# A gated delta-rule mixer ahead of a local transformer: the inversion of the delta groups split by rows over two engines, and their products rewritten with fewer, wider matmuls

## What is computed

```
T = strict_lower(-kb @ k^T) per chunk            # 32 x 32
for i in 1..31: T[i, :i] += T[i] @ T             # inverse of a triangle
T = T + I;  u = T @ v;  w = T @ kb
for each of 8 chunks:
    attn = lower(q @ k^T)
    u_i = u - w @ S
    o   = q @ S + attn @ u_i
    S   = lam * S + k^T @ u_i
stats(short), stats(long), stats(delta), stats(v)   # mean, variance, max, norm
p = floor(softmax(mlp([x, stats]) / temp))
o = p0*short + p1*long + p2*delta + p3*v
out = rms_norm(o, norm_w) @ Wo
```

## Time and profile before

| | us |
|---|---|
| median of three runs | 4124.85 |
| profiled execution | 4126.29 |
| its span | 4124.5 |
| PE busy | 3701.8 |
| DVE busy | 3111.3 |
| ACT busy | 2917.1 |
| POOL busy | 2318.9 |

### The profile page before, as it was taken

How to read it: one execution, slowest core, us unless ns; L and a number is a source line. 1 busy time by engine, 2 the same in 40 slices (tenths; PEclk the granted TensorE clock), 3 DMA queues, 4 the chain that set the end, 5 groups by cost and what they waited for, 6 DMA issues and landing times.

```text
span 4124.5 us, 143879 instructions
## 1 busy us (share of the span) xinstructions
PE 3701.8 (90%) x60178; PEld 3028.5 (73%) x60178; DVE 3111.3 (75%) x5783; ACT 2917.1 (71%) x5403; POOL 2318.9 (56%) x2139
## 2 busy tenths in 40 slices
PE   4747544799999999999999999999999999999998
PEld 3636533588887888878888888888788887888776
DVE  4385684777888777787777888777877878877873
ACT  2322121688888888888888888888888888888885
POOL 0000000666666666666666666666766666666662
PEclk9766565899999999999999999999999999999999
DMA  2000000343333333334333333333343333343332
GB/s 61 23 29 2 13 12 10 82 107 84 93 89 99 106 88 88 90 90 118 90 90 90 90 101 107 90 89 91 86 117 89 89 88 89 99 106 94 98 94 53
DMA packets 149484, 332.27 MB, mean 81 GB/s; under 512 B 17632, under 2 KB 27616, under 8 KB 147168
## 3 DMA queue, kind: packets, MB, share of 16 engines
q1 hardware_dynamic: 148832, 322.95, 29.6%
HBM read 218.02 MB, written 104.86 MB: 78 GB/s over the span
## 4 chain that ended last, share of the span: by engine, by line
PE 50%; ACT 17%; POOL 9%; issue 5%; DVE 2%; POOLq 0%; ACTq 0%; DVEq 0%
PE bank L1577 13%; PE bank L1694 8%; PE bank L1614 7%; PE bank L1667 7%; PE bank L1636 5%; PE bank L1682 3%; PE bank L1744 3%; ACT L1238 3%; ACT L1236 3%; POOL qk L1039 3%; PE bank L1651 2%; ACT gate L1236 2%; POOL qk L1049 2%; POOL pr L1058 2%; ACT qT L1132 1%
## 5 line engine op out<-in xcount | busy, mean ns | idle before, releaser
L1039 POOL TENSOR_TENSOR qk<-rot_a,rot_b 128x512 f32<-128x512 f32 x768 | 987.5, 1286 | 692.9 <-PE bank L1614 649.0
L1049 POOL TENSOR_TENSOR qk<-qk,rn 128x512 f32<-128x512 f32 x768 | 800.7, 1053 | 71.0 <-DVE rn L1456 71.0
L1377 DVE TENSOR_TENSOR rot_a<-bank,rot 128x512 f32<-128x512 f32 x768 | 531.1, 691 | 368.4 <-PE bank L1577 338.6
L1577 PE MATMUL bank<-w_hi,xs_hi 128*128 128x512 f32 x1152 | 571.8, 496 | 39.7 <-POOL xs_lo L1029 20.4
L1121 ACT ACTIVATE sq<-bank 128x512 f32<-128x512 f32 x768 | 458.9, 598 | 181.7 <-DVE rot_b L1384 179.2
L1058 POOL TENSOR_TENSOR pr<-pr,prec 128x512 f32<-128x512 f32 x384 | 400.5, 1043 | 290.4 <-DVE prec L1421 290.4
L1392 DVE TENSOR_REDUCE ss<-sq 128x8 f32<-128x512 f32 x768 | 513.9, 669 | 52.6 <-ACT sq L1121 52.4
L1384 DVE TENSOR_TENSOR rot_b<-bank,rot 128x512 f32<-128x512 f32 x768 | 522.9, 681 | 0.0
L1614 PE MATMUL bank<-ident,qk 128*128 128x128 f32 x3072 | 465.4, 274 | 53.8 <-ACT qT L1132 50.9
L1614 PEld LDWEIGHTS bank<-ident,qk 128*128 128x128 f32 x3072 | 368.5, 141 | 159.4 <-issue 92.2
L1577 PE MATMUL bank<-w_lo,xs_hi 128*128 128x512 f32 x1152 | 458.5, 398 | 0.0
(11 more groups left out here) (245 smaller groups left out, 7071.5 us busy)
## 6 DMA issues: line engine op xcount, KB each, us to landing
vw<-value_scratch SPq DMA_DIRECT2D x576, 256.0 KB, 4.9
value_scratch<-v SPq DMA_DIRECT2D x192, 512.0 KB, 2.6
vw<-value_scratch SPq DMA_DIRECT2D x192, 192.0 KB, 3.8
stage<-in_wqkv SPq DMA_DIRECT2D x6, 1536.0 KB, 8.7
stage<-in_wb_all SPq DMA_DIRECT2D x6, 1088.0 KB, 9.1
stage<-in_band SPq DMA_DIRECT2D x6, 512.0 KB, 5.1
d_xt<-in_x SPq DMA_DIRECT2D x4, 512.0 KB, 4.2
base_scratch<-d_res SPq DMA_DIRECT2D x4, 512.0 KB, 2.7
```

Of the source, the lines that this page charges most:

```text
L1039: nc.gpsimd.tensor_tensor(qk[:, c, :], rot_a[:, c % 2, :], rot_b[:, c % 2, :], ALU.add)\
L1049: nc.gpsimd.tensor_tensor(y, y, rn[:, x.q, 8 * c:8 * c + 8].unsqueeze(2).to_broadcast([P, 8, DH]), ALU.mult).then_inc(S["scaled"], 1)
L1377: nc.vector.tensor_tensor(rot_a[:, c % 2, :].rearrange("p (h d) -> p h d", h=8), proj_bank(x, c)[:, :].rearrange("p (h d) -> p h d", h=8), ...
L1577: mm = nc.tensor.matmul(out[:, :], x[:, q, half * P:(half + 1) * P], w[:, cols:cols + CK], start=n == 0, stop=n == 2)
```

## The change

- The inversion is split by the rows of `inv`. Row a depends on its own earlier columns only. GpSimd computes rows 0 to 3 (31 steps, product and add, up to 4 x (31-k) elements); VectorE computes rows 4 to 31, from k = 4 on. VectorE waits for GpSimd before it transposes.
- u and w come from one product with 64 columns (`vkb` holds both halves). Four of the eight chunks are made ahead of the scan, the other four within its first four steps. ScalarE copies u out; VectorE transposes w out of PSUM.
- The output of the scan is made by `scanned`: full-array products (128 x 128 weights, 32 columns) with `state` and `ui` laid out as block-diagonal matrices. ScalarE copies the four head blocks of `state`, GpSimd those of `ui` (4 instructions each per step). Output step n-1 is made within step n. VectorE transposes four steps at a time out of PSUM.
- The dummy products are gone.
- The statistics of v and the short filter move into the gaps of the scan on VectorE, and ScalarE's squares with them.
- The reduction over four streams becomes two adds (2048 and 1024 elements). `norm_w` is multiplied into `wout` once at the start.
- The hardware loops over the groups are written out.

```diff
+                for k in range(C - 1):
+                    n, m = min(k + 1, ROWS), C - 1 - k
+                    pr = prod_first[:, 0:n * m].rearrange("p (a b) -> p a b", a=n)
+                    nc.gpsimd.tensor_tensor(pr, na_u[:, k, k + 1:C].unsqueeze(1).to_broadcast([P, n, m]),
+                                            inv[:, 0:n, k].unsqueeze(2).to_broadcast([P, n, m]), ALU.mult).then_inc(S["inv_first"], 1)
+                    pool.wait_ge(S["inv_first"], g * 2 * (C - 1) + 2 * k + 1)
+                    nc.gpsimd.tensor_tensor(inv[:, 0:n, k + 1:C], inv[:, 0:n, k + 1:C], pr, ALU.add).then_inc(S["inv_first"], 1)
+                    pool.wait_ge(S["inv_first"], g * 2 * (C - 1) + 2 * k + 2)
...
+                for n in range(L // C):
+                    pool.wait_ge(S["ui"], g * 8 + n + 1)
+                    if n >= 2:
+                        pool.wait_ge(S["od"], g * 8 + n - 1)
+                    for h in range(H):
+                        r = slice(h * D, (h + 1) * D)
+                        nc.gpsimd.tensor_copy(ui_diag[r, n % 2, :, r], ui[r, n % 2, :, :]).then_inc(S["ui_diag"], 1)
...
-                for k in range(C - 1):
-                    n, m = k + 1, C - 1 - k
+                for k in range(ROWS, C - 1):
+                    n, m = k + 1 - ROWS, C - 1 - k
...
+                dve.wait_ge(S["inv_first"], (g + 1) * 2 * (C - 1))
...
+                sum_of(3, 4, 0)
+                turn_w(0)
+                top_of(3, 4, 0)
+                turn_w(1)
                 for n in range(L // C):
                     dve.wait_ge(S["ws"], g * 8 + n + 1)
...
+                    beside_scan(n, 0)
                     dve.wait_ge(S["sd"], g * 8 + n + 1)
...
+                    beside_scan(n, 1)
...
-                V.tensor_reduce(om[:, :, :].rearrange("p b d -> p (b d)"), cen[:, :, :].rearrange("p (s b) d -> p (b d) s", s=4),
-                                AX.X, ALU.add).then_inc(S["om"], 1)
+                V.tensor_tensor(cen[:, 0:2 * NB, :], cen[:, 0:2 * NB, :], cen[:, 2 * NB:4 * NB, :], ALU.add).then_inc(S["mixed"], 1)
+                dve.wait_ge(S["mixed"], g * 5 + 5)
+                V.tensor_tensor(om[:, :, :], cen[:, 0:NB, :], cen[:, NB:2 * NB, :], ALU.add).then_inc(S["om"], 1)
...
+                def blocks_uw(n):
+
+                    for b in range(GS):
+                        i = GS * n + b
+                        for h in range(H):
+                            r = slice(h * D, (h + 1) * D)
+                            mm = T.matmul(ps[r, 4 + i // 8, i % 8 * 2 * D:(i % 8 + 1) * 2 * D], tT[r, b * 8 + n, :], vkb[r, b * 8 + n, :],
+                                          start=True, stop=True)
...
+                def scanned(n):
+
+                    pe.wait_ge(S["ui_diag"], g * 32 + 4 * (n + 1))
+                    if n > 0:
+                        pe.wait_ge(S["state_diag"], g * 28 + 4 * n)
+                    for b in range(GS):
+                        out = ps[:, 1 + n // 4 * 2, b * P + n % 4 * C:b * P + (n % 4 + 1) * C]
+                        if n > 0:
+                            T.matmul(out, state_diag[:, n % 2, b, :], qc[:, (b * 8 + n) * C:(b * 8 + n + 1) * C], start=True, stop=False)
+                        mm = T.matmul(out, ui_diag[:, n % 2, b, :], atT[:, b * 8 + n, :], start=n == 0, stop=True)
+                    mm.then_inc(S["od"], 1)
...
+                    if n < 4:
+                        blocks_uw(n + 4)
+                    if n > 0:
+                        scanned(n - 1)
                     pe.wait_ge(S["ui"], g * 8 + n + 1)
```

More of the change, by code:

```diff
@@ L46 @@
 BAND_SLOTS = 4
+ROWS = 4
 MAGIC = float(0x5F3759DF)
@@ L238, in delta_mixer, with groups @@
             "logit", "lg", "lt", "sm_steps", "exped", "mixed", "om", "o_sq", "rms_steps", "o_norm", "oc", "out", "res",
[L239 to L245, removed]
+            "vpad_zero", "hv_act", "hv", "wout", "cen_read", "temp")}
+        def groups(group):
+            for g in range(NG):
+                group(g, g == NG - 1)
         block = stack.enter_context(nc.Block())
@@ L295, in _ @@
             nc.gpsimd.tensor_copy(wbx[:, :, :], wb[:, :].unsqueeze(2).to_broadcast([P, H, D])).then_inc(S["prep"], 1)
-            with pool.Fori(0, NG) as g:
+            for g in range(NG):
                 pool.wait_ge(S["beta"], g + 1)
@@ L427, in _ @@
             long_in(0)
-            groups(act, group)
+            groups(group)
         @block.vector
@@ new lines, in beside_scan @@
+                def beside_scan(n, half):
+                    if (n, half) == (0, 0):
+                        centre_of(3, 4, 0)
+                    if (n, half) == (0, 1):
+                        mean_out(3, 4, 0)
+                    if (n, half) == (1, 0):
+                        short_tap(0)
+                    if (n, half) == (1, 1):
+                        short_tap(1)
+                    if (n, half) == (2, 0):
+                        turn_w(2)
+                        short_tap(2)
+                    if (n, half) == (3, 0):
+                        turn_short()
+                    if (n, half) == (3, 1):
+                        dve.wait_ge(S["streams"], g * 3 + 1)
+                        sum_of(0, 1, 1)
+                    if (n, half) == (4, 0):
+                        turn_w(3)
+                    if (n, half) == (4, 1):
+                        centre_of(0, 1, 1)
+                    if (n, half) == (5, 0):
+                        mean_out(0, 1, 1)
+                        turn_scanned(0)
+                    if (n, half) == (5, 1):
+                        variance_of(3, 4, 0)
+                    if (n, half) == (6, 0):
+                        variance_out(3, 4, 0)
+                    if (n, half) == (6, 1):
+                        top_of(0, 1, 1)
+                    if (n, half) == (7, 0):
+                        variance_of(0, 1, 1)
+                    if (n, half) == (7, 1):
+                        variance_out(0, 1, 1)
@@ L642, in _ @@
             below_diagonal(0)
-            groups(dve, group)
+            groups(group)
         @block.tensor
@@ L647, in _ @@
             pe.wait_ge(S["prep"], 2)
+            pe.wait_ge(S["wout"], 1)
             pe.wait_ge(S["loaded"], 16 * NLOAD)
@@ L809, in _ @@
             long_bands()
-            groups(pe, group)
+            groups(group)
 def local_transformer(nc, stateT, ident, stage, s_wqkv, s_base, wqkv_d, scales_d, wb_d, par_d, rot_d, mask_d, v_d, base_d, out_d):
```

171 lines of the change are left out of this document (102 added, 69 removed).

## The result

The changed kernel takes 4092.5 us (median of four runs, 4092.0 to 4094.0), the kernel before 4125.4 in runs beside them: ratio 0.9919, 95% interval 0.9902 to 0.9936. It is faster by 33 us where I had forecast 17.

A forecast was written before the change was run, and what follows sets the result against it. The mixer's groups were taken as serial chains, with no stage hidden under another group. Terms +9.3 - 5 - 19.2 + 0.5 - 3.0 = -17.4 us against 4126.3 gave 4108.9 profiled, 4107 us median; range 4066 to 4138, forecast alone 4090 to 4119.

The forecast's parts named there:

- part 1: Inversion split between VectorE and GpSimd: 26.7 us, +3.1 a group, +9.3 in all; ends 22 and 34.5 us.
- rival (a): Inversion: VectorE and GpSimd exclude each other for whole instructions; 34.5 us, +10.9 a group, time 4131; chance 0.19.
- part 2: From `tT` to the projection, mainly the scan: projection starts at 49.5 instead of 50.7 us, -1.2 a group, -5 in all.
- +0.8 for collisions: Inversion: delay of GpSimd's chain by VectorE's data movement, about 0.8 us.
- 0.8 us wait for the last copies of `ui`: Last scan output: TensorE waits for GpSimd's four copies of the last `ui`, some 0.8 us past k^T u_i.
- Rival (b): Scan: wide products don't overlap load and product, or pay for tile-shape changes; at 0.65 us each 4150; chance 0.14.
- Rival (c): Scan: full-array products raise the clock above 0.50; about 4034, or 4080 if only partly; chance 0.15.
- Part 3: After the scan: reduction as two adds -3.6, norm's weight -1.2; -4.8 a group, -19.2 in all; last transpose +0.5.
- The norm's weight (-1.2): VectorE's closing chain: the multiplication by the norm's weight goes, -1.2 us a group.
- Part 4: Written-out loops: VectorE's waits of 1.80 and 1.25 us at the loop turn go, -3.0 us.

The follow-up runs named there:

- VectorE alone: Changed kernel with the inversion's split undone (ROWS = 0, GpSimd's loop gone), so VectorE inverts all 32 rows: 4090.1 us, ratio 0.9915.
- the reduction's experiment: Changed kernel with the two adds over the four streams put back as one tensor_reduce on VectorE: 4102.9 us, ratio 0.9951.

## Why the prediction came out as it did

The time, 4092.5, lies in the range and in the forecast's own span (4090 to 4119), near its lower end. The mechanism of most parts was right; the sum missed half of the gain, by the table: -11.0 of the -17.4 missing in the inversion, -3.3 in the scan, -1.9 at the start, -1.2 in the closing part.

Some of the prediction's figures don't follow from its own terms. The lower end of part 1 is 62 x 0.23 + 6.1 + 0.8 = 21.2 us, not 22, and a GpSimd wait of 0.24 us gives 33 us, not the 34.5 of rival (a). The ends of part 2 are -3.0 and +1.2 a group (60 products at 0.03 less and 0.04 more), not -3.3 and +0.7. With these the forecast's span is about 4084 to 4117; 4092.5 lies in it too. And TensorE did not fill the time from 304.7 to 321.4: it was busy 8.97 of 16.70 us.

**Part 1 failed in size and sign.** I put the split at +3.1 us a group; it is -0.5 from `na_u` to `tT` against before, of which 0.35 come with the written-out loops alone, and -0.2 against VectorE alone. That GpSimd's chain would be the longer one, and why (62 dependent steps), held. The mis-sized term is the wait between two steps of GpSimd, 0.14 us from one row of another shape and another place: it is 0.08, so 62 x 0.06 = 3.7 us too much, less 0.9 that the steps themselves took longer. The +0.8 for collisions was 0.1. My lower end lay nearer.

**The rival (a)**, exclusion of whole instructions, fell. The Trainium skill's page SBUF — State Buffer (section Who interferes with whom) lets VectorE or GpSimd hold the port for a whole instruction; by that the inversion would last 34.5 us. It lasted 23.2, and GpSimd's part 23.05 us beside VectorE and 22.97 alone; here the measurement decides. In the short steps here the one that pays is VectorE, 2.6 us in 54 operations.

**Part 2** had the right place and nearly the right price: a wide product 0.43 us (I took 0.47, and my lower end was 0.44), a late step 5.3 us (5.4), clock 0.50. Its four groups were not alike, though: -0.9, -2.7, -2.8 and -2.0 us from `tT` to the statistics. The 0.8 us wait for the last copies of `ui` didn't exist: `scanned(7)` began 0.58 us after the first of its k^T u_i products, as any products in a row. So 47.9 instead of 49.5. The Trainium skill's page TensorE: Matmul & The Clock Gate (section LDWEIGHTS) gives 107 ns for 128 columns, and the traces come near that at full clock alone: 0.21 us for two passes at 1.00 and 0.25 for a wide product in the reduction's experiment, against 0.43 us at 0.50 here. That columns and not rows are paid, as the prediction has the trace agree, its rows can't tell: their weights are 128 x 128 or 32 x 32, and differ in both.

What I did not ask in part 2 was the better question. I compared the wide products with the old step, dummies and exposed drains included, and found them about even. The right comparison is with small products in the same new order, and there the wide form loses 52 us. It was visible in my own terms: 3.8 us against 32 x 0.03 = 1.0 for a chunk. That is three times the gain I forecast.

**Rival (b)** (changes of tile shape cost) has a mechanism that fits the runs, 0.3 us for a pair of changes, but the changed kernel makes one pair a chunk and so pays little. **Rival (c)** did not come: the clock is 0.50 through the wide products. It did rise ahead of them, for a few us, behind a run of small products with 64 columns, so the reason that (c) gives for 0.50, only small tiles at work, doesn't hold; and where wide products met 1.00 (the reduction's experiment) it was back at 0.50 with the next ones (595 to 598: 0.51). For the changed kernel, second group:

```profile
294.70:298.00 3.30, 3.25 (x115) 3.11 (x119) 2.94 (x5) 0.38 (x1) 0.00 (x0) 0.50 0.02 5
298.00:301.50 3.50, 2.15 (x126) 1.75 (x121) 3.31 (x8) 0.40 (x2) 1.53 (x2) 0.85 0.02 5
301.50:307.00 5.50, 4.62 (x148) 4.11 (x152) 2.33 (x5) 1.98 (x7) 2.27 (x7) 0.58 0.02 3
307.00:343.00 36.00, 33.45 (x529) 31.80 (x521) 14.15 (x31) 10.76 (x27) 7.77 (x24) 0.50 0.01 2
```

**Part 3** held as written: the adds take 2.29 + 1.23 us, and the second group's closing chain with the turn is 6.2 us shorter (4.8 and 1.25 forecast); putting the reduction back cost 10.4 of its 14, and the rest came back by the clock at least in part. The norm's weight (-1.2) had no experiment. **Part 4** was small: 3.0 forecast, 5.6 to 7 measured by itself, as a written-out loop also shortens stretches in which no turn lies.

## What to carry to other kernels

Before a dependent chain is split by elements, multiply its number of steps by the fixed price of a step on the slower engine: here 62 steps at 0.28 us and more made a third of the elements as long as the whole. Cutting GpSimd's steps from 62 to 40 by another choice of rows took 0.9 us off an inversion and no more, since VectorE then had the 62 steps; the rest of that kernel's gain lies elsewhere. Compare a new form of an operation with the other forms it could have in the new order, not with the old kernel's step, of which waits and fillers are a part. For fp32 products with 32 columns at clock 0.50, one with full-size weights took 0.43 us and four small tiles side by side a quarter of it (0.11), as long as the small ones came in runs and TensorE did not stand between them. And before a gain of a few us is put down to an edit, compare the granted clock in the stretches that it didn't touch.

## What the runs showed of the hardware

- GpSimd's tensor_tensor took 0.20 us for 4 elements a partition and 0.38 for 112, and a step that waits for the one before started 0.08 us after it.
- Alternating 32 x 32 and 128 x 128 tiles cost TensorE about 0.3 us for the way there and back, at clock 0.50 (a price of summing across the shapes, if there is one, included).
- An fp32 product with 128 x 128 weights and 32 columns took 0.43 us at clock 0.50 and 0.25 at 1.00.
- A scan with 128 small matmul records a step ran at 3.3 to 4.8 us a step, with single waits of up to 1.9 us that no semaphore explains, and work added to it cost about twice its running time.
- Small products at 90% and wide products at 93% of the time both left the granted clock at 0.50; the same projection, behind the same scan, met 0.72 or 0.50 in its first 3 us in two kernels, and four wide products at the same place met 1.00 or 0.50. What decides is open.
